# SyncE gathers one chunk of 128 rows in every twelve units instead of every thirty, by byte offsets loaded sixteen at a time

## The reference: what is computed

```python
h = relu(layernorm(x))
x = x + L0(h)     # attention, 3 edge types: w = exp(leaky(a_s[src] + a_d[dst]) - max over dst), sum of w * xw[src] / sum of w
h = relu(layernorm(x))
x = x + L1(h)     # convolution: messages = (h[src] @ dW + db) * (silu(edge_attr @ fW1 + fb1) @ fW2 + fb2)
                  # aggregated = segment_sum(messages, dst); upd = silu(aggregated @ uW1 + ub1) @ uW2 + ub2
```

## Time and profile before

| What | us |
|---|---|
| Median of 3 runs | 5422.99 (5419.43 to 5437.17) |
| Span of the profiled execution, first to last instruction | 4155.8 |
| What lies around the span, the median less the span | 1267.2 |
| Attention gathers, first to last start | 61.1 to 2066.5 |
| Convolution gathers, first to last start | 2114.1 to 4122.9 |

### The profile page before, as it was taken

The page is one execution under the profiler, slowest core; times in us unless marked ns, Lnnn a source line. Parts: engine busy times, 40 slices in busy tenths (PEclk is TensorE's granted clock), DMA queues, the critical chain, the costliest instruction groups (busy, mean ns, idle before and its releaser), DMA issues.

```text
span 4155.8 us, 58597 instructions
## 1 busy us (share of the span) xinstructions
PE 3395.1 (82%) x13945; PEld 2624.2 (63%) x13946; DVE 2388.6 (57%) x5253; ACT 1364.7 (33%) x3361; POOL 3070.8 (74%) x3239
## 2 busy tenths in 40 slices
PE   5788788888888888888777888888888888788888
PEld 3566666666666666666555666666666666667666
DVE  7888888888888888888842322322332323223223
ACT  5455555555555555555411111111111111111111
POOL 5777777777777777777657777777777777777775
PEclk7555555555555555555577666676666666766667
DMA  4222222222222222222223222222222222222222
GB/s 124 56 59 61 59 59 61 60 59 61 59 59 61 59 59 61 59 59 61 58 60 98 77 74 76 71 76 75 71 76 73 74 75 72 75 76 71 76 74 79
DMA packets 180619, 286.01 MB, mean 69 GB/s; under 512 B 82273, under 2 KB 123054, under 8 KB 176011
## 3 DMA queue, kind: packets, MB, share of 16 engines
q0 software_dynamic: 102656, 213.73, 19.6%
q1 hardware_dynamic: 77856, 71.32, 6.1%
HBM read 271.06 MB, written 12.49 MB: 68 GB/s over the span
## 4 chain that ended last, share of the span: by engine, by line
POOL 36%; issue 12%; POOLq 1%; PE 1%; DMA 0%; DVE 0%; DVEq 0%
POOL ce_xg L63 36%; POOLq L676 0%; PE ce_ring L1429 0%; PE ce_ps_h L1420 0%; PE ce_ring L1420 0%; POOLq L677 0%; PE ce_ps_h L1407 0%; POOLq L688 0%; PE ce_ring L1385 0%; DMA ce_xg<-table,ce_idx 0%; POOLq L1275 0%; DVE ce_msg L1466 0%; POOLq L686 0%; DVE sums L1519 0%; DVEq L1275 0%
## 5 line engine op out<-in xcount | busy, mean ns | idle before, releaser
L63 POOL DMA_INDIRECT ce_xg<-table,ce_idx x1604 | 1520.8, 948 | 498.4 <-issue 488.9
L63 POOL DMA_INDIRECT ae_xg<-table,ae_idx x1604 | 1517.5, 946 | 501.8 <-issue 501.5
L1466 DVE TENSOR_TENSOR ce_msg<-ce_ring,ce_xg 128x768 f32<-128x768 f32 x269 | 257.7, 958 | 1333.7 <-DMA ce_xg<-table,ce_idx 1333.3
L924 PE MATMUL ae_ps_k<-ae_xg,ae_e 128*96 128x129 f32 x3224 | 882.4, 432 | 0.0
L1397 PE MATMUL ce_ps_h<-ce_ea,ce_fw 50*128 50x384 f32 x1076 | 611.9, 706 | 258.3 <-DMA ce_ea<-in_edge_attr 257.3
L1339 ACT ACTIVATE ce_hid<-ce_ps_h,ce_fb 128x768 f32<-128x768 f32 x269 | 242.5, 901 | 1749.6 <-PE ce_ps_h L1397 1749.6
L924 PEld LDWEIGHTS ae_ps_k<-ae_xg,ae_e 128*96 128x96 f32 x3224 | 689.4, 277 | 126.5 <-issue 117.1
L1376 PEld LDWEIGHTS ce_ring<-ce_fw,ce_hid 128*128 128x128 f32 x3228 | 582.2, 276 | 290.4 <-issue 151.8
L1376 PE MATMUL ce_ring<-ce_fw,ce_hid 128*128 128x128 f32 x3228 | 650.9, 376 | 65.5 <-DVE ce_msg L1466 65.4
L1385 PEld LDWEIGHTS ce_ring<-ce_hot,ce_msg 128*128 128x128 f32 x3224 | 521.1, 250 | 4.4 <-DVE ce_msg L1466 4.2
L1385 PE MATMUL ce_ring<-ce_hot,ce_msg 128*128 128x32 f32 x3224 | 507.3, 316 | 2.5 <-DVE sums L1474 2.5
(11 more groups left out here) (181 smaller groups left out, 3235.8 us busy)
## 6 DMA issues: line engine op xcount, KB each, us to landing
ce_ea<-in_edge_attr SPq DMA_DIRECT2D x90, 450.0 KB
ae_xg<-table,ae_idx POOLq DMA_INDIRECT x1604, 2.5
ce_xg<-table,ce_idx POOLq DMA_INDIRECT x1604, 2.5
ae_stage<-table SPq DMA_DIRECT2D x1024, 0.5 KB
ce_stage<-table SPq DMA_DIRECT2D x1024, 0.5 KB
sums<-in_x SPq DMA_DIRECT2D x7, 448.0 KB, 5.1
table<-sums SPq DMA_DIRECT2D x6, 462.0 KB, 3.6
pj_bias<-in_x_rows SPq DMA_DIRECT2D x42, 64.0 KB
```

Source lines behind the costliest of these rows:

```text
L63: eng.indirect_dma_start(out=out, out_offset=None, in_=table[:, :], in_offset=bass.IndirectOffsetOnAxis(ap=idx, axis=0)).then_inc(done, 16)
L924: last = nc.tensor.matmul(ps_k[0:KEYS, 0:D + 1], by_chunk[s % 3][:, c, :], xg[:, s % XS, c, 0:D + 1], start=(c == 0), stop=(c == count - 1))
L1466: nc.vector.tensor_tensor(msg[:, s % 3, :, :], filt, xg[:, s % XS, :, :], ALU.mult).then_inc(s_msg, 1)
```

## The change

- `SPAN` becomes 2 and `CARRIED` 20: the last chunk of slot 4 of turns 2, 4, ... 40 is carried, one in twelve units.
- All lists of a stage (20 x 128 source numbers) are fetched in one DMA into one partition, ahead of the loops. They are multiplied by the row's size in bytes on the chip, once per stage: by GpSimd at the end of `prepare` for the attention, by VectorE at the start of the convolution stage. `read_list` and its wait go.
- `collect` loads 16 offsets at a time instead of 8 and addresses the table as a flat array of bytes, so a row's offset needs no multiplication. A half turn has 128 / 4 = 32 rows.
- In the attention stage the two stores, with their wait for the mask, move behind the rows of that half turn (`behind`). The wait that the delivered chunk has landed also moves behind the rows.
- `carry_turns` and `gather_units` write out the turns before the first span and the two turns of a span where they had inner loops.

```diff
+def row_starts(state):
+    return state[96:97, 0, 0:CARRIED * P].bitcast(i32)
...
# prepare, SyncE and GpSimd
             first_indices(sp, a, sources.idx, sources.idx_in)
+            sp.dma_start(row_starts(state), a["src_rows"][:, :]).then_inc(lists_in, 16)
             project.load_rows(sp, a)
...
                     nc.gpsimd.tensor_copy(typ[:, :, :], raw[:, :, :])
+            pool.wait_ge(lists_in, 16)
+            nc.gpsimd.tensor_scalar(row_starts(state), row_starts(state), 4.0 * ROW, None, ALU.mult)
             pool.wait_ge(s_steps, 3)
...
-SPAN = 5
-SPANS = TURNS // SPAN
-CARRIED = SPANS - 1
+SPAN = 2
+CARRIED = 20
 CARRY_SLOT = 4
+READ = 16
...
-def carry_turns(eng, body, apart=0):
+def carry_turns(eng, body):
     body(0, True, SL, 0)
-    for i in range(1, apart + 1):
-        body(i, False, SL, 0)
-    with eng.Fori(apart + 1, SPAN) as i:
-        body(i, False, SL, 0)
-    with eng.Fori(1, CARRIED) as t, eng.Fori(0, SPAN) as j:
+    for i in range(1, 2 * SPAN):
+        body(i, False, SL, i // SPAN)
+    with eng.Fori(2, CARRIED) as t, eng.Fori(0, SPAN) as j:
         body(SPAN * t + j, False, SL, t, j)
...
-    def read_list(self, sp, a, chunk, b):
-        sp.dma_start(self.lists[:, b, :], a["src_rows"][bass.ds(chunk - 1, 1), :]).then_inc(self.list_in, 16)
-    def collect(self, nc, sp, table, b, q):
-        todo = range(q * P // (SPAN * LOADS), (q + 1) * P // (SPAN * LOADS))
-        for first in range(todo[0], todo[-1] + 1, 8):
-            part = range(first, min(first + 8, todo[-1] + 1))
-            rows = nc.values_load_multi_w_load_instructions(
-                self.lists[:, b, part[0]:part[-1] + 1], engines=[mybir.EngineType.SP], min_val=0, max_val=N - 1,
+    def collect(self, nc, sp, t, b, q):
+        share = P // (SPAN * LOADS)
+        size = 4 * self.width
+        for first in range(q * share, (q + 1) * share, READ):
+            starts = nc.values_load_multi_w_load_instructions(
+                self.lists[:, bass.ds(t * P + first, READ)], engines=[mybir.EngineType.SP], min_val=0, max_val=(N - 1) * size,
                 skip_runtime_bounds_check_because="a source is a node")[1]
-            for p, row in zip(part, rows):
-                sp.dma_start(self.stage[p:p + 1, b, :], table[bass.ds(row, 1), :]).then_inc(self.rows_in, 16)
+            for p, start in enumerate(starts, first):
+                sp.dma_start(self.stage[p:p + 1, b, :].bitcast(u8), self.bytes[:, bass.ds(start, size)]).then_inc(self.rows_in, 16)
...
# load_indices, one span
             following(r, SPAN * t + j, v)
-            if q == 0:
-                if not first:
-                    deliver(r, t, b)
-                sp.wait_ge(carry.list_in, 16 * (r * CARRIED + t + 1))
-                carry.read_list(sp, a, t + 2, b)
-                if not first:
-                    sp.wait_ge(carry.carried, 16 * (r * CARRIED + t))
-                    sp.sem_inc(carry.turn, 1)
-            carry.collect(nc, sp, table, 1 - b, q)
+            if q == 0 and not first:
+                deliver(r, t, b)
+            if q == 0 and first:
+                listed()
+            carry.collect(nc, sp, t, 1 - b, q)
+            if v == 0:
+                behind(r, SPAN * t + j)
+            if q == 0 and not first:
+                sp.wait_ge(carry.carried, 16 * (r * CARRIED + t))
+                sp.sem_inc(carry.turn, 1)
...
# gather_units
-        with pool.Fori(1, SPAN) as i:
+        for i in range(1, SPAN):
             turn(i, False, SL)
-        with pool.Fori(1, SPANS - 1) as t:
+        with pool.Fori(1, CARRIED) as t:
             turn(SPAN * t, False, SL, t)
-            with pool.Fori(1, SPAN) as j:
+            for j in range(1, SPAN):
                 turn(SPAN * t + j, False, SL)
...
# attention, SyncE: the two stores leave beside
                     sp.dma_start(p.x[:, :], a["x_rows"][bass.ds((i - OPEN) * P, P), :]).then_inc(x_in, 16)
+            def behind(r, i):
                 if closes(i):
                     sp.wait_ge(s_masked, r * UNITS + i * SL + 3)
                     sp.dma_start(messages[bass.ds((i - OPEN - 1) * P, P), :], p.turned).then_inc(stored, 16)
...
# convolution, SyncE and VectorE
+            sp.dma_start(lists[:, :], a["src_rows"][:, :]).then_inc(lists_in, 16)
             update.load(sp, a)
...
             nc.vector.memset(acc[:, :], 0.0).then_inc(cleared, 1)
+            dve.wait_ge(lists_in, 16)
+            nc.vector.tensor_scalar(lists[:, :], lists[:, :], 4.0 * D, None, ALU.mult).then_inc(scaled, 1)
             dve.wait_ge(cleared, 2)
```

More of the change, by code:

```diff
@@ L57 @@
 fp32, bf16 = mybir.dt.float32, mybir.dt.bfloat16
-i32, u16 = mybir.dt.int32, mybir.dt.uint16
+i32, u16, u8 = mybir.dt.int32, mybir.dt.uint16, mybir.dt.uint8
 ALU, ACT, AX = mybir.AluOpType, mybir.ActivationFunctionType, mybir.AxisListType
@@ L576, with __init__ @@
 class Carry:
-    def __init__(self, sb, sem, width, project, lists):
+    def __init__(self, sb, sem, width, project, lists, table):
         self.width = width
@@ L582, in __init__ @@
         self.lists = lists
[L583 removed]
+        self.bytes = table.rearrange("n r -> (n r)").rearrange("(o x) -> o x", o=1).bitcast(u8)
+        self.rows_in, self.carried = sem("rows_in"), sem("carried")
         self.turn = project.carry_turn
@@ L648, in load_indices @@
         span(r, 0, 0, True)
-        with sp.Fori(0, CARRIED // 2 - 1) as p:
+        span(r, 1, 1)
+        with sp.Fori(1, CARRIED // 2) as p:
+            span(r, 2 * p, 0)
             span(r, 2 * p + 1, 1)
-            span(r, 2 * p + 2, 0)
-        span(r, CARRIED - 1, 1)
-        for q in range((SPAN - 1) * LOADS):
+        for q in range((TURNS - 1 - SPAN * CARRIED) * LOADS):
             j, v = divmod(q, LOADS)
             following(r, SPAN * CARRIED + j, v)
+            if v == 0:
+                behind(r, SPAN * CARRIED + j)
             if q == 0:
                 deliver(r, CARRIED, 0)
+        sp.wait_ge(carry.carried, 16 * (r + 1) * CARRIED)
+        sp.sem_inc(carry.turn, 1)
         for v in range(LOADS):
@@ L661, in load_indices @@
         beside(r, TURNS - 1)
+        behind(r, TURNS - 1)
     for v in range(LOADS):
         sp.wait_ge(idx_in[v], 16 * (passes * TURNS + 1))
-    sp.wait_ge(carry.list_in, 16 * (passes * CARRIED + 1))
     sp.sem_inc(landed, 1)
@@ L779, in _ @@
             sp.sem_inc(stored, 32)
-            load_indices(nc, sp, a, h, idx, idx_in, gathered, landed, carry, table, xg, s_sum, beside=beside)
+            load_indices(nc, sp, a, h, idx, idx_in, gathered, landed, carry, xg, s_sum, beside=beside, behind=behind)
             passes = pass_count(sp, h)
@@ L1187, in _ @@
                 dve.wait_ge(project.moved, 16 * (NT + 1))
-                carry_turns(dve, turn, OPEN)
+                carry_turns(dve, turn)
                 base = bases(nc, mybir.EngineType.DVE, h, UNITS - 3, 3)
@@ L1294, in convolution_edges @@
         ea_in = [sem(f"ea_in{v}") for v in range(LOADS)]
-        carry = Carry(sb, lambda name: sem("c_" + name), D, project, sb("lists", [1, 2, P], i32))
+        lists, lists_in, scaled = sb("lists", [1, CARRIED * P], i32), sem("lists_in"), sem("scaled")
+        carry = Carry(sb, lambda name: sem("c_" + name), D, project, lists, table)
         (w_in, pool_turn, steps, key_ready, begun, cleared, s_hid, s_act, s_flt, s_bias, s_msg, s_sum, s_acc) = (
@@ L1317, in attributes @@
                              a["edge_attr_50"][:, 0:10, bass.ds((i * LOADS + v) * LOAD * UE, LOAD * UE)]).then_inc(ea_in[v], 16)
-            load_indices(nc, sp, a, h, sources.idx, sources.idx_in, gathered, sem_landed, carry, table, xg, s_msg, attributes)
+            load_indices(nc, sp, a, h, sources.idx, sources.idx_in, gathered, sem_landed, carry, xg, s_msg, attributes, listed=lambda: sp.wait_ge(scaled, 1))
             with sp.Fori(0, GROUPS - 1) as g:
```

14 lines of the change are left out of this document (7 added, 7 removed).

## The result

The changed kernel takes 5566.9 us (median, 5559.2 to 5573.41), the kernel before in the same comparison 5424.01 us (5419.43 to 5437.17). The ratio is 1.0264 [1.0241, 1.0286]: slower by 143 us, where 30 us less were forecast.

What follows compares the result with a forecast made beforehand. The prediction took GpSimd's back-to-back gathers to bound both stages. Gathers removed (-30.0 us) and an added list DMA (+0.4) made -29.6 us, all else nothing: 5423.0 to 5393.4 us, range 5376 to 5416, with 73%.

Steps and rivals of the forecast that it cites:

- What lies around the span (1267 us): Timed run outside the profiled span: taken as unchanged, so 5423.0 us falls by 29.6 to 5393.4.
- if POOL waits for `idx_in`: Sign in the changed profile that the prediction is wrong: GpSimd waits for the indices SyncE loads.
- Its own alternative: Whole kernel: if the 1267 us came from everything being slower in the timed runs, the gain would be 39 us.
- What bounds the kernel: Both stages: GpSimd goes from one gather to the next, 1.251 and 1.253 us apart; VectorE follows.
- Gathers removed, 30.0 us: Both stages: 12 fewer gathers in each take 30.0 us off the path, bounds 22.7 and 30.0.
- SyncE's added work: SyncE's queue, both stages: 78.5 of 89.0 us in a span of two turns, so 1536 more rows cost nothing.
- the prediction's 0.50 us for a row: SyncE's span against 71 gathers: row price from which SyncE would become the bound.
- The rival: SyncE's span against 71 gathers: SyncE becomes the bound, 5439 us with rows at 0.51, 5755 with dear loads; 9%.
- Sharing of the DMA engines: Gathers beside SyncE's row DMAs: no slowdown taken, bounds 0 and 6 us.
- the moved steps: SyncE's half turn: two stores some 18 us later and the delivered chunk's wait behind the rows delay nobody.
- Scaling the lists: Stage starts: 7.2 us on GpSimd, 2.9 on VectorE, both hidden; bounds 0 to 3.4 and 0 to 2.9 us.
- VectorE takes over in the attention: Attention: rival that VectorE sets the pace and the stage gains nothing, 5408 us; 8%. Otherwise its waits fall to 134 us.

Runs made afterwards that it cites:

- e15: Changed kernel with 640 instead of 2560 row transfers in a stage, each fetching four neighbouring rows: 5357.33 us against 5418.97 for the kernel before, ratio 0.9875.
- e16: Changed kernel, unchanged, in the same job as e15: 5589.06 us against 5418.97 for the kernel before, ratio 1.0314.
- e3: Changed kernel, unchanged, where the kernel before takes 4153.32 us: 4123.47 us, ratio 0.9928.
- e0: Kernel before, unchanged, profiled beside timed runs: one execution of 4156.39 us with a span of 4154.6 us.
- e10: Kernel before with 304 instead of 1024 row transfers in a stage: 5465.10 us against 5481.36 for the kernel before, ratio 0.9969.
- e2: Changed kernel with a quarter of the row transfers, 640 instead of 2560 in a stage: 4127.04 us against 4155.56 for the kernel before, ratio 0.9929.
- e7: Changed kernel with the two stores and the delivered chunk's wait in front of the 32 rows again: 4125.06 us against 4154.13 for the kernel before, ratio 0.9936.
- e6: Changed kernel with row numbers, loads of 8 and the table addressed by row: 4123.72 us against 4154.13 for the kernel before, ratio 0.9927.

## Why the prediction was wrong

**The step that failed** is the sum's last: "What lies around the span (1267 us) is taken as unchanged". There is nothing around the span. The span of 4155.8 us and the median of 5423 belong to two conditions of the machine, and the prediction priced everything in one to forecast the other. The term that was wrong by it is "SyncE's 1536 more rows in a stage cost nothing": it took a row at 0.416 us, in the runs that were timed a row took 0.82 us in the convolution, GpSimd waited 546.6 us for its indices there, and the transfers cost 203 us of that stage (e15 against e16). Of its own signs of being wrong the first came true: "if POOL waits for `idx_in`". Its own alternative, that everything is slower in the timed runs and the gain 39 us, failed too: a gather takes 944 ns in both (e3, after); SyncE's rows (0.33 to 0.81 us) and signals from TensorE to VectorE become dear, and so the bound changes.

**What bounds the kernel.** Gathers from one to the next, in both stages: right for the profile shown and for e0, e3. At the longer time the consumers hold the attention, and SyncE the changed kernel's convolution. That they also hold the kernel before there is argued from e10, which has fewer transfers; the kernel before itself was never profiled there.

**Gathers removed, 30.0 us**: right at the shorter time (29.9; that it fits to a tenth is luck, the interval of e3 is 24 to 36 us). So was the choice of start-to-start distance over the gather's own 947 ns, which gave 22.7: e3's gathers stand 1.249 and 1.254 us apart.

**SyncE's added work, hidden**: right at the shorter time. The row was taken at 0.416 us and measured 0.33; the load of 16 at 2.2 and measured 1.14 to 1.29; SyncE waited a third of each stage (686.6 of 1987 us), not a tenth. At the longer time the row took 0.82 us in the convolution: 128 x 0.82 = 105 us for rows alone in a span, with 8 loads and the rest at the prices of the shorter time (9 and 8 us) an estimated 122; 4 x 30.9 = 124 were measured. But 89 us is not the measure there, and so neither is the prediction's 0.50 us for a row: the consumers give SyncE 4 x 28.4 = 114 us (e15). In the attention rows took 0.72 us, well over 0.50, and the stage was no longer for it. The rival had this mechanism, with 9%, but priced it from rows up to 0.51 us.

The price of 2.2 us for a load had a wrong reading behind it, which did no harm. Half of the loads of the kernel before bring only 4 or 5 values, so that half of all take under 1.35 us says nothing of those with 8 (nor against the 1.6 us). Told apart in its trace, the loads of 8 that begin at a multiple of four values in the list take 0.70 to 1.09 us, the others 1.85 to 2.36; of 5 values 0.69 to 0.97 and 1.31 to 1.41. The long ones go with where they begin; no run changes that alone. A load of 16 in the changed kernel always begins at a multiple of 16.

**Sharing of the DMA engines, the moved steps**: nothing, and so measured (e2, e7). **Scaling the lists**: GpSimd's timeline at the start of the attention in e3:

```profile
49.18 6.68 POOL L256 TENSOR_SCALAR state<-state 1x2560 int32<-1x2560 int32 x1
62.12 1.17 POOL L63 DMA_INDIRECT ae_xg<-table,ae_idx  x1 [6.26 <-issue]
```

And VectorE's at the start of the convolution:

```profile
2098.99 1.42 DVE L1465 TENSOR_SCALAR ce_lists<-ce_lists 1x2560 int32<-1x2560 int32 x1
```

6.68 us for 7.2, hidden with 6.26 us of idle time behind it; 1.42 us for 2.9. **VectorE takes over in the attention**: no; it waits 122.3 us for gathers (L1112) where 134 were forecast.

**No version beats both everywhere.** The changed kernel wins 0.7% at the shorter time and loses 2.6 to 3.6% at the longer. Fewer transfers for the same rows would win in both (e2, e15), but only because those experiments leave out the rows' own sources. SPAN = 4 was not met by the longer time.

**What stays open** is what makes the longer time: why SyncE goes in steps of 0.70 us for some stretches, and why TensorE's signals are late in the same runs. Both conditions have the same instructions, bytes and gather times. TensorE's mean granted clock is lower at the longer time (0.557 against 0.598 in e3), but over the attention it is 0.50 (the 1.2 GHz level) in both, and the stage is longer all the same: 2619 against 1987 us. So the clock isn't what makes that stage longer. In the convolution it is 0.60 against 0.68, and what that costs there isn't parted from the rest. Nor is it known how much of the loss of 143 us lies in which stage, since the kernel before has no profile at the longer time.

## What to carry to other kernels

Before any sum, compare the profiled execution's own time with the timed runs; where span and median don't fit, the prices are those of another condition than the one that is timed, and a forecast should say what each queue's work costs if its price doubles. An engine that is "free" at 88% of its span is free only at those prices. Here it was a queue of many small transfers that became dear, and a quarter of the transfers for the same bytes took 232 us off (5589 to 5357, e16 and e15). A threshold such as "from 0.50 us for a row" is worth stating beside the chance, with what it rests on: it told at the shorter time that the change would fit (e3), but the span of 89 us in it belongs to that condition as much as the prices do.

## What the runs showed of the hardware that was not expected

- One program on one chip (chip 1) took 4158.65 and, in the next job, 5481.36 us, 1.32 times, with gathers as long as before (944 and 947 ns).
- In the longer condition SyncE's 528 byte transfers cost 0.72 us and its 512 byte ones 0.82 from start to start in the mean, instead of 0.33, and this in stretches with steps of 0.70 us. GpSimd's gathers show no such change.
- A register load from SBUF takes 0.43 us for one value, 0.64 for two, 0.46 for four and 1.14 for sixteen: two cost more than four. The Trainium skill, "Runtime: NRT & Kernel Launch", section "Instruction fetch mechanics", gives some 200 ns for each register even in bulk, where registers are loaded from HBM; that would be an estimated 3.2 us for sixteen. These loads read SBUF, and there the traces don't agree: 1.14 / 16 is 71 ns each.
- Where a load begins counts as much as its length: 8 values from a multiple of four in the list 0.70 to 1.09 us, from elsewhere 1.85 to 2.36, and in e6, from multiples of eight, 0.69 in the middle. No run changes the beginning alone.
- The same 2560 int32 products in one partition take 6.68 us on GpSimd and 1.42 us on VectorE.
